# Two transformer layers on one core: storing the token table first, zeroing 32 slot tiles inside the first expert loop, and making the attention's key tables in six pieces

## The reference

```python
x = x + tanh(g_xattn[0]) * L0_xattn(layernorm(x), ctx, ...)   # linear attention
x = x + tanh(g_ffn[0])   * L0_ffn(layernorm(x), ...)          # 8 experts, 2 a token, and a shared one
x = x + tanh(g_xattn[1]) * L1_xattn(layernorm(x), ctx, ...)   # 16 heads over 512 keys
x = x + tanh(g_ffn[1])   * L1_ffn(layernorm(x), ...)          # 16 experts, 4 a token, and a shared one

# L0_ffn, on 2048 rows
shared = (silu(x @ sw_gate) * (x @ sw_up)) @ sw_down
top_w, top_i = top_k(softmax(x @ router_w.T), 2); top_w /= top_w.sum(-1)
h = silu(x @ w_gate[e]) * (x @ w_up[e]);  routed = sum_e combine[:, e] * (h @ w_down[e])
out = routed + sigmoid(x @ shared_gate_w) * shared

# L1_xattn: q, k and v are rounded to 127 levels per head (v per column), the softmax to 255
attn = fq_unsigned(softmax(fq(q * scale) @ fq(k).T)); out = (attn @ fq(v)) @ Wp + bp
```

## Time and profile before

| | us |
|---|---|
| runs, median (lowest to highest of 3) | 927.02 (926.72 to 927.92) |
| profiled execution, span from first to last instruction | 924.4 |
| PE, DVE, POOL, ACT busy, share of the span | 78%, 74%, 55%, 48% |
| mean share of the 16 DMA engines, q1 (SP's transfers) and q0 (POOL's gathers) | 40.8%, 12.7% |

### The profile page before, as it was taken

One profiled execution on the slowest core, in us unless ns is written; L12 is line 12 of the kernel. 1 busy time (PEld: TensorE's weight loads), 2 busy tenths in 40 slices (PEclk: granted clock), 3 DMA queues, 4 the chain that ended last, 5 costly groups with the idle time before them and its releaser, 6 DMA issues.

```text
span 924.4 us, 18404 instructions
## 1 busy us (share of the span) xinstructions
PE 725.4 (78%) x5700; PEld 487.8 (53%) x5701; DVE 682.8 (74%) x1825; ACT 440.6 (48%) x1037; POOL 505.8 (55%) x607
## 2 busy tenths in 40 slices
PE   3469747678999798577788777668699999999990
PEld 1258635356675355244444444344567777775650
DVE  4968957756775776999988999648867777773574
ACT  3365415323332123699888999634033344342330
POOL 5284894547663838555553557010164444468885
PEclk9678975979999899779877887758989999999995
DMA  8034444724443211599999999820034444455445
GB/s 297 1 88 152 145 143 155 231 75 132 146 147 104 82 56 46 112 182 177 192 175 196 200 185 179 151 91 8 10 113 139 131 131 137 139 151 120 80 92 154
DMA packets 205754, 121.17 MB, mean 131 GB/s; under 512 B 146476, under 2 KB 197808, under 8 KB 205680
## 3 DMA queue, kind: packets, MB, share of 16 engines
q1 hardware_dynamic: 192816, 91.10, 40.8%
q0 software_dynamic: 12864, 29.14, 12.7%
HBM read 64.16 MB, written 32.98 MB: 105 GB/s over the span
## 4 chain that ended last, share of the span: by engine, by line
PE 27%; POOL 9%; DVE 9%; ACT 9%; issue 7%; DMA 4%; DVEq 2%; POOLq 1%; ACTq 0%; SPq 0%
PE PS L269 13%; ACT sb_xnf L1417 4%; PE PS L852 4%; POOL sb_region L713 4%; DVE sb_wk L1450 3%; DMA sb_xnf<-sb_xnf 3%; ACT sb_wkh L1417 3%; PE PS L791 2%; POOL sb_stg L713 2%; PE PS L815 2%; PE PS L844 2%; PE PS L1344 2%; POOL sb_xnf L713 1%; PE PS L407 1%; POOL sb_wqp L713 1%
## 5 line engine op out<-in xcount | busy, mean ns | idle before, releaser
L673 POOL DMA_INDIRECT sb_xnf<-token_table,sb_ids x120 | 115.9, 966 | 149.1 <-DVE sb_wk L1018 63.1
L1450 DVE TENSOR_SCALAR_CACHE_REDUCE sb_wk<-PS 128x512 f16<-128x512 f32 x256 | 161.7, 684 | 8.2 <-PE PS L1344 7.6
L269 PE MATMUL PS<-sb_xnT,sb_sgu 128*128 128x512 f16 x528 | 126.2, 391 | 1.1 <-DVE sb_lg L455 0.6
L269 PE MATMUL PS<-sb_region,sb_wkh 128*128 x720 | 120.2, 318 | 5.6 <-issue 3.2
L875 ACT ACTIVATE sb_wk<-PS 128x512 f32<-128x512 f32 (+1 forms) x48 | 28.6, 596 | 140.8 <-PE PS L269 128.1
L269 PEld LDWEIGHTS PS<-sb_region,sb_wkh 128*128 128x128 f16 x720 | 68.8, 99 | 46.7 <-issue 14.6
L1417 ACT ACTIVATE sb_xnf<-PS,sb_slotv 128x512 int16<-128x512 f32 x128 | 87.0, 704 | 11.9 <-DVE sb_wk L1450 7.9
L1417 ACT ACTIVATE sb_wkh<-PS,sb_slotv 128x512 int16<-128x512 f32 x128 | 87.4, 707 | 10.8 <-DVE sb_wk L1450 8.7
L269 PEld LDWEIGHTS PS<-sb_xnT,sb_sgu 128*128 128x128 f16 x528 | 52.4, 100 | 58.7 <-issue 7.5
L791 PE MATMUL PS<-sb_sdn,sb_wkh 128*128 128x256 f16 x544 | 69.4, 279 | 16.9 <-DVE sb_wkh L989 15.1
L1018 DVE SCALAR_TENSOR_TENSOR sb_wk<-PS,sb_sm,sb_wk 128x176 f32<-128x176 f32 x120 | 42.6, 397 | 52.7 <-ACT sb_wk L903 52.6
(11 more groups left out here) (296 smaller groups left out, 1682.3 us busy)
## 6 DMA issues: line engine op xcount, KB each, us to landing
slot_table<-sb_wa SPq DMA_DIRECT2D x60, 256.0 KB
slot_table<-token_table SPq DMA_DIRECT2D x16, 640.0 KB
sb_stg<-gu SPq DMA_DIRECT2D x24, 352.0 KB, 4.1
sb_stg<-dn SPq DMA_DIRECT2D x24, 256.0 KB, 3.6
token_table<-sb_xnf SPq DMA_DIRECT2D x16, 256.0 KB, 4.8
sb_stg<-sgu SPq DMA_DIRECT2D x8, 352.0 KB, 5.3
sb_x_sb<-x SPq DMA_DIRECT2D x1, 2048.0 KB, 12.2
out<-sb_x_sb SPq DMA_DIRECT2D x16, 128.0 KB, 2.5
```

What stands on the lines that cost most here:

```text
L269: last = nc.tensor.matmul(out_, lhs(i, c), rhs(j, c), start=(c == 0 and n == 0 and not begun), stop=(c == C - 1 and n == 2 and not more))
L673: nc.gpsimd.indirect_dma_start(xg[l][:, 2 * (g % XR) + n, :], None, xw[l][:, :], bass.IndirectOffsetOnAxis(ap=ids[:, 2 * g + n:2 * g + n + ...
L1450: nc.vector.tensor_scalar(h_any[(2 * s + h) % 6], PS[:, (2 * s + h) % LB, :], LEVELS, None, ALU.add, ALU.min, accum_out=h_nb[s % 3][:, h:h ...
```

## The change

`zero_slots` now clears two tiles instead of five, and only the last 32 tiles of the 80. It is no longer called between the loads of the experts, but by `rows_dma` of layer 0, after each of the first 16 stores of the loop, on the same queue. `table_dma` comes right after the loads of the experts, ahead of all eight loads of layer-1 weights. `keys_apart` becomes six pieces: two copies on ACT (steps 4 and 6), two clears of `kT_odd` on DVE (steps 3 and 5) and two clears of `kT` on DVE (steps 7 and 10), with a new semaphore `p_kodd` from the copies.

```diff
--- before.py
+++ after.py
@@ -644,13 +644,13 @@
         def zero_fill(sp, l):
             sp.dma_start(xw[l][T // 2:T // 2 + P, :], zero[:, 0:PK[l]]).then_inc(zeroed[l], 16)
 
-        ZERO_PARTS = 16
+        ZERO_PARTS, ZERO_TILES = 16, 2
 
         def zero_slots(sp, n):
 
-            tiles = NS[1] // ZERO_PARTS
-            sp.dma_start(ys[1][n * tiles * P:(n + 1) * tiles * P, :].rearrange("(n p) d -> n p d", p=P),
-                         xw[1][T // 2:T // 2 + P, 0:D].unsqueeze(0).broadcast_to([tiles, P, D])).then_inc(table_zeroed, 16)
+            first = (NS[1] - (ZERO_PARTS - n) * ZERO_TILES) * P
+            sp.dma_start(ys[1][first:first + ZERO_TILES * P, :].rearrange("(n p) d -> n p d", p=P),
+                         xw[1][T // 2:T // 2 + P, 0:D].unsqueeze(0).broadcast_to([ZERO_TILES, P, D])).then_inc(table_zeroed, 16)
 
         def rows_dma(sp, l):
             for g in range(NG[l]):
@@ -659,6 +659,10 @@
                              yb[g % 2].rearrange("p (n d) -> p n d", n=2)).then_inc(e_st[l][g % 2].sem, 16)
                 if l == 0 and g % 3 == 1 and g // 3 < LOOP_ITEMS:
                     load_item(sp, FIRST_ITEMS + 4 + g // 3)
+                if l == 0 and g == 0:
+                    sp.wait_ge(zeroed[1], 16)
+                if l == 0 and g < ZERO_PARTS:
+                    zero_slots(sp, g)
 
         def out_dma(sp):
             for t in range(NT):
@@ -1061,7 +1065,7 @@
 
 
         p_v = sem("p_v"); p_vq = sem("p_vq"); p_vT = sem("p_vT"); p_sv = sem("p_sv"); p_wh = sem("p_wh")
-        p_k = sem("p_k"); p_kq = sem("p_kq"); p_kT = sem("p_kT"); p_kd = sem("p_kd"); p_kpad = sem("p_kpad"); p_kf = sem("p_kf"); p_ks = sem("p_ks")
+        p_k = sem("p_k"); p_kq = sem("p_kq"); p_kT = sem("p_kT"); p_kd = sem("p_kd"); p_kpad = sem("p_kpad"); p_kodd = sem("p_kodd"); p_kf = sem("p_kf"); p_ks = sem("p_ks")
         q_xn = sem("q_xn"); q_xT = sem("q_xT"); q_xh = sem("q_xh"); q_xl = sem("q_xl"); q_ps = sem("q_ps")
         q_frac = sem("q_frac"); q_int = sem("q_int"); q_T = sem("q_T"); q_ready = sem("q_ready")
         h_qk = sem("h_qk"); h_max = sem("h_max"); h_exp = sem("h_exp")
@@ -1208,17 +1212,23 @@
                                             .rearrange("p (g n) -> p g n", n=P), ACT.Copy, scale=-1.0)
             last.then_inc(p_kd, 1)
 
-        def keys_apart(dve):
-            at_least(dve, p_kd, 0, KT)
+        def tables_free(eng):
+
             for u in range(2):
-                at_least(dve, e_st[0][u], 0, 16 * len(range(u, NG[0], 2)))
-            nc.vector.memset(kT_odd[0:P // 2], 0.0)
-            for i in range(2):
-                nc.vector.tensor_copy(kT_odd[P // 2:P, 4 * i:4 * i + 4, :], kT[i][P // 2:P])
-            dve.drain()
-            for i in range(2):
-                last = nc.vector.memset(kT[i][P // 2:P], 0.0)
-            last.then_inc(p_kpad, 1)
+                at_least(eng, e_st[0][u], 0, 16 * len(range(u, NG[0], 2)))
+
+        def odd_keys_act(act, i):
+            at_least(act, p_kd, 0, KT)
+            tables_free(act)
+            nc.scalar.activation(kT_odd[P // 2:P, 4 * i:4 * i + 4, :], kT[i][P // 2:P], ACT.Copy).then_inc(p_kodd, 1)
+
+        def odd_zeros_dve(dve, i):
+            tables_free(dve)
+            nc.vector.memset(kT_odd[0:P // 2, 4 * i:4 * i + 4], 0.0)
+
+        def even_zeros_dve(dve, i):
+            at_least(dve, p_kodd, 0, i + 1)
+            nc.vector.memset(kT[i][P // 2:P], 0.0).then_inc(p_kpad, 1)
 
         def deviations_dve(dve, n, first, end):
             dve.wait_ge(rstd_ready, n)
@@ -1299,6 +1309,8 @@
                 query_transposes(pe, 0)
 
         def ahead_act(act, i):
+            if i in (4, 6):
+                odd_keys_act(act, (i - 4) // 2)
             if i == 8:
                 queries_act(act, 0)
             if i == 13:
@@ -1307,8 +1319,10 @@
         def ahead_dve(dve, i):
             if i == 6:
                 deviations_dve(dve, 3, 0, EARLY)
-            if i == 5:
-                keys_apart(dve)
+            if i in (3, 5):
+                odd_zeros_dve(dve, (i - 3) // 2)
+            if i in (7, 10):
+                even_zeros_dve(dve, (i - 7) // 3)
             if i == 7:
                 nc.vector.memset(q_i[:, :, :, 3, :], 0.0)
             if i == 9:
@@ -1375,7 +1389,8 @@
                     last.then_inc(o_y, 1)
 
             at_least(pe, s_h[0], 0, NSH)
-            pe.wait_ge(p_kpad, 1)
+            pe.wait_ge(p_kpad, 2)
+            pe.wait_ge(p_kodd, 2)
             for s in range(AHEAD):
                 logits(s)
             at_least(pe, s_accr[0], 0, BLK)
@@ -1635,15 +1650,10 @@
                     de = a["dn0"][e] if isinstance(base, int) else a["dn0"][e, :, :].rearrange("o h n -> (o h) n")
                     load(2 * k, (base, 2 + s), ge.rearrange("(c p) n -> p c n", c=C), 2 * EG)
                     load(2 * k + 1, (base, 2 + s), de.rearrange("(c p) n -> p c n", c=2), 2 * D)
-            sp.wait_ge(zeroed[1], 16)
             for s in range(E[0] // 2):
                 two_experts(0, s)
-                for n in range(4):
-                    zero_slots(sp, 4 * s + n)
-            for n in range(4):
-                load_item(sp, n)
             table_dma(sp, 0)
-            for n in range(4, FIRST_ITEMS + 4):
+            for n in range(FIRST_ITEMS + 4):
                 load_item(sp, n)
             rows_dma(sp, 0)
             for n in range(LATER_ITEMS + 4, BEFORE_KEYS + 4):
```

## The result

The changed kernel takes **972.12 us** (median of 4 runs, 968.67 to 974.83) against 927.05 of the kernel before beside it: ratio 1.047, 95% interval [1.044, 1.050], slower. The forecast was 959.7 us with a range of 938 to 972: the sign is right, and so is the mechanism of the large term; the size is 12 us short, and the median lies 0.1 us past the upper end. The profiled run is one of 970.55 us with a span of 968.8, 44.4 more than the span before.

What follows compares the result with a forecast made beforehand. PE sets the first expert loop's pace; with the change, two DMA engines working on zeros become its bound. Terms 36.5 - 6.3 + 2.5 = +32.7 on a span of 924.4, plus 2.6 around it, gave 959.7 us, range 938 to 972.

Steps and rivals of the forecast that it cites:

- The zeros in the loop: First expert loop: stores queue behind zeros on two DMA engines; loop ends 36.5 us later, start's 4.0 gain included.
- The reading of the DMA share: 35% busy while five-tile zeros run alone: one engine per tile, so a two-tile zero still takes 5.34 us.
- The group's 7.0 us: First expert loop: zero, store, gathers and load on the two engines take 7.0 us a group, against 4.06.
- Table first: Start, before the first gather: earlier power and table store bring the first store 4.0 us earlier.
- that wait goes too: 4.0 us together: Routing: DVE's 2.34 us wait for the stored table vanishes besides the power's 1.7 us; 4.0 us gained.
- The 1.7 us of a late power: Start: POOL's power, at 136.11 us though statistics are there at 134.33, comes on time; 1.7 us fall away.
- The wait of 2.34 us: Routing: DVE's wait for the stored table before its first comparison, L572, claimed to disappear.
- Six pieces: End of the shared expert: splitting `keys_apart` sums to -6.3 us, ends -3 and -8.
- the low half comes 4.7 us earlier: End of the shared expert: with one smaller clear before it, DVE's low half 4 comes 4.7 us earlier.
- Half clock at the start of that stage: End of the shared expert: PE, idle some 5 us before it, starts at half clock; +2.5 us, ends 0 and 3.
- Attention, layer 1 and the output are untouched: Stages after the shared expert: no change, since their zeros are long written; 0 us.
- the zeros are cheap: Rival, first loop: two tiles take 2.14 us of queue, no store is late; 916.7, up to 923 us; chance 10%.

Runs made afterwards that it cites:

- rows outermost: Changed kernel with the same 16 two-tile zeros in the same places, but the 128 rows as outermost dimension instead of the tiles: 932.7 us, 1.005.
- keys-only kernel: Kernel before with the attention key tables in six pieces and nothing else of the change: 929.91 us, 1.003.
- held-up transposes: Changed kernel's two-tile, tiles-outermost zeros moved behind the first loop, ahead of the attention's first transposes; against the kernel before: 980.2 us, 1.059.

## Why the prediction was right, and where it was short

- **The zeros in the loop** (+40.5 forecast, +41.9 measured). Right in mechanism and size. The reading of the DMA share, one engine for one tile, is borne out by zeros of two, four and 16 tiles, by both shapes and by 24 GB/s an engine with two, five and 16 at work. The group's 7.0 us was 6.85. The loop ended at 333.5, not near 327, since it began 4.6 us later than forecast and took 1.4 more, 1.0 of it the last down product at half clock, which the sum had at full clock. Left out of the sum was what the zeros do to the gathers: POOL's drains took 24.3 us instead of 14.9, which the wait for stores hides here, and rows outermost brings to light.
- **Table first** (-4.0 forecast, +0.6 measured). The failed step is "that wait goes too: 4.0 us together". The 1.7 us of a late power were the slack of an execution in which the attention ended early, at 134.16, against 137.36 when the same kernel was profiled again. The wait of 2.34 us did go, but DVE's own work just ahead of L572 and behind it grew, which the forecast took to stay as it was. The first gather comes at 191.1 to 192.9 us in the six profiles with the old start, at 190.9 to 192.5 in the eight with the new one: the new order is worth nothing that these runs can show.
- **Six pieces** (-6.3 forecast; -2.5 with the half clock at the start, and nothing in the keys-only kernel). The failed step is "the low half comes 4.7 us earlier". It counted what leaves step 5 and put the pieces of steps 3, 7 and 10 beside waits of DVE. But DVE bounds these steps up to some 328 us: of its work only the two copies of 0.69 us have left it, and the clears of steps 3, 5 and 7 delay the low half or the shared sum there. The prediction priced the clear of step 7 at 0.9 us; the gap it stands in grew from 1.75 to 3.29 and 3.86 us.
- **Half clock at the start of that stage** (+2.5 forecast). 36 products took 9.24 us instead of 7.93: 1.3.
- **"Attention, layer 1 and the output are untouched"** (0 forecast, +4.4 measured). It was priced at nothing, and the +2.6 of layer 1 is more than the two profiles of before differ by. One more instruction of PE ahead of the loop, which the change brings, is the likely cause of a part of it: alone it made the kernel before 0.3% slower. The rest and the way it acts stay open, since the loop took 153.8 and 155.5 us in two kernels without it. The +1.8 of the attention and its routing is within its scatter (293.4 to 300.1 us in the kernels without held-up transposes).

The rival *the zeros are cheap* needed 16 engines for two tiles; rows outermost gives it just that. No store is then late, and the loop's 5.9 us, with POOL's drains 4.5 us longer, lie within the 6 us that the rival allowed. That it comes to 932.7 and not to 916.7 to 923 is due to the gains of the start and the keys, which the rival shared with the forecast and which were not there.

## What to carry to other kernels

Look at the outermost dimension of a DMA before its bytes: a copy of two tiles with the tiles outermost holds up everything behind it on its queue for as long as one engine needs for a whole tile, and moving it only changes who waits. Before you take a wait in a profile for a gain, look at a second execution, and ask whether the work ahead of it and behind it stays as long when the wait is gone. And before you cut a blocking piece of work into parts, count the engine's whole work over these steps: a part moved to another busy step moves the wait, a part moved to an idle one removes it.

## What had not been expected of the hardware

- **A DMA engine copies at one pace, alone or beside 15 others.** 24.0 GB/s each with two at work, 24.4 with five and 23.9 with 16, for rows of 1 KB from DRAM to DRAM. What changes with the shape is how many work: two tiles of 128 KB move at 48 GB/s with the tiles outermost.
- **One long-fulfilled wait on PE costs 0.3%** of the kernel before (930.18 us, 1.003 [1.001, 1.005]). Its layer-1 loop, nearly 300 us further on and with the same instructions, took 156.38 us, against 153.04 and 153.19; but 155.54 is seen without such a wait too.
- **Small DVE operations beside POOL's splits** take 0.2 us or 0.7 to 1.5, and which of them is slow changes from one execution to the next: L554 took 0.18 us and L555 1.50 in the first profile of before, 0.78 and 0.17 in the second and in the changed kernel.
